# Layer 0: scores in four banks, two transpose banks and two rotating banks, with a new order of the row on every engine

## The chip, the cores and the metric

The kernel runs on one core of one Trainium2 chip. The metric is the time of one execution in microseconds of that core. The core has five engines with instruction queues of their own: TensorE (PE in the profile; its weight loads are PEld), VectorE (DVE), ScalarE (ACT), GpSimd (POOL) and SyncE (SP), which issues all DMA here. Each works through its queue in order; they meet only at semaphores. Matmuls write to PSUM, which has eight banks of 128 partitions by 512 float32; VectorE and ScalarE read them, GpSimd can't.

## What is computed

An image x of 128 channels by 256 by 256 goes through two residual layers, each behind a group normalisation. The change touches layer 0 alone: attention along each of the 256 rows of the image, with 4 heads of 64 channels, a bias per head, a gate and an output projection.

```python
x = (pair_rep - mu) * jax.lax.rsqrt(var + EPS) * ln_w + ln_b
q = proj(wq); k = proj(wk); v = proj(wv)          # (heads, 64, rows, 256)
g = jax.nn.sigmoid(proj(wg_w) + wg_b)
bias = jnp.einsum('hc,bcij->bhij', wb, x)
scores = jnp.einsum('bhcij,bhcik->bhijk', q, k) * scale + bias[:, :, None, :, :]
a = jax.nn.softmax(scores, axis=-1)
o = g * jnp.einsum('bhijk,bhcik->bhcij', a, v)
return jnp.einsum('oc,bcij->boij', wrep_w, o) + wrep_b
```

## The kernel before

The program has a first pass over the image (statistics and the bias parts, to about 426 us), layer 0, a short end of statistics, and layer 1. Layer 0 walks over the 256 image rows, W = 256 positions each, eight rows to an iteration of the loop (`UNROLL`). Every number of the products that feed scores is held as a high and a low part (float32r), and a product of two such numbers is three matmuls (`matmul_split`: high by high, low by high, high by low). One image row is:

- GpSimd: `normalise` parts 0 to 5, which subtract the mean, scale, weight, shift, and split into xn high and low; `divide`, which multiplies each head's exponents by the inverse of their sum. SyncE loads x, ln_w and ln_b in tiles of two rows into four buffers; a buffer is loaded again when its rows' y is done, since the residual reads x from it.
- TensorE: `queries`, `keys`, `values`, `gates` (6 matmuls of 128x256 each); `scores` per pair of heads (12 matmuls on half the array's height, two side by side); `transposes` per head (4 of 128x128); `attend` (8 matmuls in the program, 16 in the records, on half the array's width); `project_out` (6).
- ScalarE copies the high part of q and k (`queries_high`, `keys_high`), v (`values_out`), the tanh of the gates (`gates_out`), the high part of o, two heads' transposes, and the exponents with their sums.
- VectorE adds the bias to the scores and takes the maximum (`biased`), inverts the sums, subtracts for the low parts of q, k and o, copies two heads' transposes, multiplies by the gate (`gated`), adds the residual (`residual`, y) and measures y for the next statistics (`measure`). In the eight rows after iterations 7, 14, 21 and 28 it also joins the statistics of seven iterations (`join`).

The order on each engine is written by hand in its function `row(t, k, has)`: `scores(t, k + 2, 0)` in it means that in step k of the engine's walk the scores are those of image row k + 2. So each kind of work runs a fixed number of rows ahead, and the steps before row 0 and behind row 255 leave out what doesn't exist. The exponents lie in one buffer per head (`probs`), q, k, v, the gate and the transposed exponents in two each. The banks before: one for queries and values, one for keys and gates, two for scores (so the second pair of heads waits until the first pair has been read), two for transposes, one for attend, one for the output projection. A block's wait names who must have read its bank:

```python
for h in range(2):
    if pair:
        pe.wait_ge(s_ready[h], r + 1)
    else:
        wait(pe, s_ready[2 + h], r)
```

## Time and profile before

| | us |
|---|---|
| median of 3 runs (4820.17 to 4829.05) | 4822.93 |
| the profiled execution | 4825.53 |
| its span, first to last instruction | 4823.7 |
| TensorE busy, matmuls | 4606.1 (95%) |
| TensorE busy, weight loads | 3896.8 (81%) |
| VectorE busy | 3924.8 (81%) |
| ScalarE busy | 3768.1 (78%) |
| GpSimd busy | 3626.7 (75%) |
| TensorE's granted clock, mean | 0.975 of full speed |

The span is the profiled execution from its first instruction to its last; the execution's own time is 1.8 us longer. Busy shares are means over four stages with different limits, so what the change is worth has to be read inside layer 0, from about 440 to 2842 us. A granted clock of 1.00 is 2.4 GHz, 0.50 is 1.2 GHz. Idle time of an engine is printed behind an instruction in brackets with what ended it. A matmul's start is recorded and its end is modelled.

### The profile page before, as it was taken

What the parts mean: (1) busy time and instruction counts of PE and PEld (TensorE: products, weight loads), DVE (VectorE), ACT (ScalarE), POOL (GpSimd) and SP (SyncE); (2) the same over time, 40 slices, a digit from 0 to 9 for tenths busy, and PEclk for the clock granted to TensorE, in tenths of its full rate; (3) what the DMA queues carried; (4) which work ended last, traced back from release to release, by engine and by line L of the source; (5) the groups of instructions that cost most, each with busy time, mean ns of one, the idle gap of its engine ahead of it and who ended that gap; (6) DMA issues with size and microseconds to landing.
All of it is one profiled execution on the core that took longest, in us unless ns stands there. A gap on an engine that the chain in (4) does not pass through costs nothing. (4 is left out here: it accounts for less than half of the span.)

```text
span 4823.7 us, 153371 instructions
## 1 busy us (share of the span) xinstructions
PE 4606.1 (95%) x46135; PEld 3896.8 (81%) x46135; DVE 3924.8 (81%) x12976; ACT 3768.1 (78%) x11664; POOL 3626.7 (75%) x6054
## 2 busy tenths in 40 slices
PE   5667999999999999999999989999999999999998
PEld 1225888888888888888888868888888888888887
DVE  4444888889888988898888968888888888888887
ACT  2336888888888888888888868888888888888886
POOL 3443888888888888888888847777777777777776
PEclk8678999999999999999999989999999999999999
DMA  9996111111111111111111111111111111111111
GB/s 355 351 346 198 58 53 61 52 61 52 61 52 61 53 57 56 53 60 52 61 52 61 53 45 48 52 52 52 52 52 52 52 52 52 52 52 52 52 52 34
DMA packets 237387, 383.12 MB, mean 79 GB/s; under 512 B 18756, under 2 KB 156616, under 8 KB 224968
## 3 DMA queue, kind: packets, MB, share of 16 engines
q1 hardware_dynamic: 237256, 381.63, 23.3%
q8 instruction: 51, 0.84, 0.1%
q14 instruction: 80, 0.66, 0.0%
HBM read 309.21 MB, written 72.35 MB: 79 GB/s over the span
## 5 line engine op out<-in xcount | busy, mean ns | idle before, releaser
L1507 POOL TENSOR_SCALAR l_probs<-l_probs,l_inv 128x256 f32<-128x256 f32 x2048 | 941.5, 479 | 377.5 <-DVE l_inv L1404 377.5
L663 POOL TENSOR_SCALAR l_probs<-l_probs,l_inv 128x256 f32<-128x256 f32 x2048 | 947.8, 477 | 268.5 <-DVE l_inv L914 268.5
L832 ACT ACTIVATE l_probs<-l_probs,l_neg_max 128x256 f32<-128x256 f32 x2048 | 1021.0, 518 | 0.8 <-DVE l_neg_max L906 0.6
L1305 ACT ACTIVATE l_probs<-bank,l_neg_max 128x256 f32<-128x256 f32 x2048 | 942.5, 476 | 46.4 <-DVE l_neg_max L1398 39.4
L906 DVE CUSTOM_DVE_ANT_0 l_probs<-bank,bias 128x256 f32<-128x256 f32 x2048 | 779.9, 418 | 201.1 <-PE bank L773 197.1
L1411 DVE TENSOR_TENSOR l_probs_t<-bank,bias 128x512 f32<-128x512 f32 x1024 | 669.7, 685 | 131.0 <-PE bank L1217 116.0
L1398 DVE TENSOR_REDUCE l_neg_max<-bank 128x2 f32<-128x512 f32 x1024 | 675.0, 682 | 43.1 <-PE bank L1205 33.9
L773 PE MATMUL bank<-ident,l_probs 128*128 128x128 f32 x4096 | 629.5, 276 | 1.1 <-POOL l_probs L663 0.7
L1217 PE MATMUL bank<-ident,l_probs 128*128 128x128 f32 x4096 | 560.0, 274 | 5.3 <-POOL l_probs L1507 3.9
L786 PE MATMUL bank<-l_probs_t,l_v 128*64 128x256 f32 x4096 | 498.5, 385 | 0.2 <-issue 0.2
L773 PEld LDWEIGHTS bank<-ident,l_probs 128*128 128x128 f32 x4096 | 463.9, 141 | 36.8 <-POOL l_probs L663 1.7
L1217 PEld LDWEIGHTS bank<-ident,l_probs 128*128 128x128 f32 x4096 | 458.7, 141 | 25.1 <-POOL l_probs L1507 5.9
L872 ACT ACTIVATE l_probs_t<-bank 128x512 f32<-128x512 f32 x512 | 308.4, 602 | 212.7 <-PE bank L773 212.7
L832 ACT ACTIVATION_READ_ACCUMULATOR l_probs<-l_probs,l_neg_max 128x1 f32 x2048 | 428.9, 209 | 0.0
L1305 ACT ACTIVATION_READ_ACCUMULATOR l_probs<-bank,l_neg_max 128x1 f32 x2048 | 424.6, 207 | 0.0
L928 DVE COPY l_probs_t<-bank 128x512 f32<-128x512 f32 x512 | 350.1, 684 | 50.7 <-PE bank L773 50.5
L786 PEld LDWEIGHTS bank<-l_probs_t,l_v 128*64 128x64 f32 x4096 | 271.5, 136 | 143.4 <-issue 0.4
L675 POOL TENSOR_TENSOR l_xf<-l_x,mean 128x256 f32<-128x256 f32 x256 | 302.1, 1180 | 70.4 <-DMA l_ln_b<-in_L_conv_ln_b_dram 70.4
L97 PE MATMUL bank<-l_xn_high,wqk_high 128*128 128x256 f32 x1024 | 331.2, 323 | 14.4 <-POOL l_xn_low L690 14.1
L760 PE MATMUL bank<-l_k_high,l_q_high 64*128 64x256 f32 x2048 | 342.2, 331 | 1.5 <-DVE l_k_low L922 1.5
L531 POOL TENSOR_TENSOR fp_ln_w<-fp_x,fp_ln_w 128x2048 f32<-128x2048 f32 x32 | 144.3, 4509 | 219.1 <-PE bank L415 219.1
L760 PEld LDWEIGHTS bank<-l_k_high,l_q_high 64*128 64x128 f32 x2048 | 191.5, 184 | 142.4 <-issue 142.1
(205 smaller groups left out, 14710.2 us busy)
## 6 DMA issues: line engine op xcount, KB each, us to landing
fp_x<-in_x_dram SPq DMA_DIRECT2D x32, 1024.0 KB, 6.4
fp_ln_w<-in_L_conv_ln_w_dram SPq DMA_DIRECT2D x32, 1024.0 KB, 8.5
fp_ln_b<-in_L_conv_ln_b_dram SPq DMA_DIRECT2D x32, 1024.0 KB, 11.1
fp_pair<-in_L_conv_pair_repr_dram SPq DMA_DIRECT2D x32, 1024.0 KB, 10.6
l_x<-in_x_dram SPq DMA_DIRECT2D x128, 256.0 KB, 2.9
l_ln_w<-in_L_conv_ln_w_dram SPq DMA_DIRECT2D x128, 256.0 KB, 3.3
l_ln_b<-in_L_conv_ln_b_dram SPq DMA_DIRECT2D x128, 256.0 KB, 3.5
x<-l_y SPq DMA_DIRECT2D x128, 256.0 KB, 2.0
```

Source lines behind the costliest of these rows:

```text
L663: last = nc.gpsimd.tensor_scalar(probs[:, h, c], probs[:, h, c], inv[:, h, c:c + 1], 1.0, ALU.mult, ALU.mult)
L760: last = nc.tensor.matmul(b_s[j][:, c * W:(c + 1) * W], q[a][channels, k % 2, pair, c * P:(c + 1) * P], kk_[b][channels, k % 2, pair], sta ...
L773: last = nc.tensor.transpose(b_t[h % 2][:, kc * W + qc * P:kc * W + (qc + 1) * P], probs[:, h, qc, kc * P:(kc + 1) * P], m.ident[:])
L786: last = nc.tensor.matmul(b_av[D0 * j:D0 * (j + 1), pair * W:(pair + 1) * W], v[:, k % 2, kc, h * D0:(h + 1) * D0], probs_t[:, k % 2, h, k ...
L832: last = nc.scalar.activation(probs[:, h, c], probs[:, h, c], ACT.Exp, bias=neg_max[:, h, c:c + 1], scale=-1.0, accum_out=total[:, h, c:c ...
L906: last = nc.vector.tensor_tensor_reduce(out=probs[:, h, c], in0=b_s[h % 2][:, c * W:(c + 1) * W], in1=m.bias0[:, c, h], scale=-1.0, scalar ...
L928: nc.vector.tensor_copy(probs_t[:, k % 2, h], b_t[h % 2][:].rearrange("p (a c) -> p a c", a=KC)).then_inc(t_ready[h], 1)
L1217: last = nc.tensor.transpose(b_t[h % 2][:, kc * W + qc * P:kc * W + (qc + 1) * P], probs[:, h, qc, kc * P:(kc + 1) * P], m.ident[:])
L1305: last = nc.scalar.activation(probs[:, h, c], b_s[h % 4][:, c * W:(c + 1) * W], ACT.Exp, bias=neg_max[:, h, c:c + 1], accum_out=total[:, h ...
L1398: nc.vector.tensor_reduce(neg_max[:, h], b_s[h % 4][:].rearrange("p (a c) -> p a c", a=KC), AX.X, ALU.max, negate=True).then_inc(max_ready, 1)
L1411: nc.vector.tensor_tensor(probs_t[:, k % 2, h], b_t[h % 2][:].rearrange("p (a c) -> p a c", a=KC), m.bias1[:, :, h], ALU.add).then_inc(t_r ...
L1507: last = nc.gpsimd.tensor_scalar(probs[:, h, c], probs[:, h, c], inv[:, h, c:c + 1], 1.0, ALU.mult, ALU.mult)
```

## The change

Banks: four for scores, two for transposes, and two that rotate: queries, keys and the output projection share b_r[0]; values, gates and attend share b_r[1]. TensorE scores all four heads of a row in one stretch. Attend no longer stands behind the values but by itself between keys and transposes. Queries run four rows ahead of the output projection and keys five (both three before), GpSimd's first part seven rows (five before). Every engine has a new order. The numbers and shapes of the instructions stay the same. The lines of the kernel after are up to 33 lines further down than those of the same work before (L760 becomes L788, L773 L799, L786 L817).

The core of the diff (the other blocks' waits are changed in the same way; VectorE's and GpSimd's orders are new as a whole):

```diff
-    AHEAD = 5
+    AHEAD = 7
+    TURN_BANK = (0, 1, 0, 1)
+    TURNED_AHEAD = ((2, 1), (3, 1), (0, 0), (1, 0))
...
-        b_qv, b_kg = m.psum[0], m.psum[1]
-        b_s, b_t, b_av, b_out = m.psum[2:4], m.psum[4:6], m.psum[6], m.psum[7]
+        b_r, b_s, b_t = m.psum[0:2], m.psum[2:6], m.psum[6:8]
...
             def gates(t, k):
                 r = UNROLL * t + k
-                pe.wait_ge(k_ready, r + 1)
+                pe.wait_ge(xn_ready, r + 1)
+                if exists(r):
+                    pe.wait_ge(v_ready, r + 1)
...
             def scores(t, k, pair):
...
-                for h in range(2):
-                    if pair:
-                        pe.wait_ge(s_ready[h], r + 1)
-                    else:
-                        wait(pe, s_ready[2 + h], r)
+                for h in range(2 * pair, 2 * pair + 2):
+                    wait(pe, s_ready[h], r)
...
             def transposes(t, k, h):
...
-                if h >= 2:
-                    pe.wait_ge(t_ready[h - 2], r + 1)
-                else:
-                    wait(pe, t_ready[h + 2], r)
+                ahead, rows_back = TURNED_AHEAD[h]
+                wait(pe, t_ready[ahead], r + 1 - rows_back)
...
             def attend(t, k):
...
-                wait(pe, o_ready, r)
+                if exists(r + 1):
+                    pe.wait_ge(g_ready, r + 2)
...
             def project_out(t, k):
                 r = UNROLL * t + k
                 pe.wait_ge(o_split, r + 1)
-                wait(pe, y_ready, r)
+                if exists(r + 4):
+                    pe.wait_ge(q_ready, r + 5)
...
             def row(t, k, has):
-                if has(2):
-                    scores(t, k + 2, 0)
...
+                if has(4):
+                    queries(t, k + 4)
+                if has(2):
+                    values(t, k + 2)
                 if has(3):
-                    queries(t, k + 3)
...
+                    scores(t, k + 3, 0)
+                    scores(t, k + 3, 1)
                 if has(0):
                     project_out(t, k)
-                if has(3):
-                    values(t, k + 3)
+                if has(2):
+                    gates(t, k + 2)
+                    transposes(t, k + 2, 3)
+                    transposes(t, k + 2, 0)
+                if has(5):
+                    keys(t, k + 5)
                 if has(1):
                     attend(t, k + 1)
+                if has(3):
+                    transposes(t, k + 3, 1)
+                if has(2):
+                    transposes(t, k + 2, 2)
             rows(pe, row)
```

TensorE in the middle of an iteration before, from head 2's transposes (bank 4) over the keys to the scores; the brackets name the semaphores that an instruction waits for:

```order
L773 MATMUL bank4<-ident,l0_probs 128x128 [waits l0_t_ready0,l0_p_ready2]
L773 MATMUL bank4<-ident,l0_probs 128x128 x3
L97 MATMUL bank1<-l0_xn_high,wqk_high 128x256 [waits l0_g_ready,l0_xn_ready]
L98 MATMUL bank1<-l0_xn_low,wqk_high 128x256
L99 MATMUL bank1<-l0_xn_high,wqk_low 128x256
L97 MATMUL bank1<-l0_xn_high,wqk_high 128x256
L98 MATMUL bank1<-l0_xn_low,wqk_high 128x256
L99 MATMUL bank1<-l0_xn_high,wqk_low 128x256
L773 MATMUL bank5<-ident,l0_probs 128x128 [waits l0_t_ready1,l0_p_ready3]
L773 MATMUL bank5<-ident,l0_probs 128x128 x3
L760 MATMUL bank2<-l0_k_high,l0_q_high 128x256 [waits l0_s_ready0,l0_s_ready1,l0_k_ready,l0_q_ready]
```

And after, from the last matmul of the gates over the transposes of heads 3 and 0 and the keys to attend:

```order
L99 MATMUL bank1<-l0_xn_high,wg_t_low 128x256
L799 MATMUL bank7<-ident,l0_probs 128x128 [waits l0_t_ready1,l0_p_ready3]
L799 MATMUL bank7<-ident,l0_probs 128x128 x3
L799 MATMUL bank6<-ident,l0_probs 128x128 [waits l0_t_ready2,l0_p_ready0]
L799 MATMUL bank6<-ident,l0_probs 128x128 x3
L97 MATMUL bank0<-l0_xn_high,wqk_high 128x256 [waits l0_y_ready,l0_xn_ready]
L98 MATMUL bank0<-l0_xn_low,wqk_high 128x256
L99 MATMUL bank0<-l0_xn_high,wqk_low 128x256
L97 MATMUL bank0<-l0_xn_high,wqk_high 128x256
L98 MATMUL bank0<-l0_xn_low,wqk_high 128x256
L99 MATMUL bank0<-l0_xn_high,wqk_low 128x256
L817 MATMUL bank1<-l0_probs_t,l0_v 64x256 [waits l0_t_ready3,l0_v_ready,l0_t_ready2,l0_g_ready,l0_t_ready1,l0_t_ready0]
```

The transposes that stood apart stand in one stretch, and behind the keys comes attend, which waits for all four transposes, v, and the gates of the next row.

TensorE around the scores before, from the last matmuls of pair 0 on:

```order
L760 MATMUL bank3<-l0_k_low,l0_q_high 128x256
L760 MATMUL bank2<-l0_k_high,l0_q_low 128x256
L760 MATMUL bank3<-l0_k_high,l0_q_low 128x256
L773 MATMUL bank4<-ident,l0_probs 128x128 [waits l0_t_ready2,l0_p_ready0]
L773 MATMUL bank4<-ident,l0_probs 128x128 x3
L97 MATMUL bank1<-l0_xn_high,wg_t_high 128x256 [waits l0_k_ready]
```

And after, where pair 0 (banks 2 and 3) meets pair 1 (banks 4 and 5):

```order
L788 MATMUL bank3<-l0_k_low,l0_q_high 128x256
L788 MATMUL bank2<-l0_k_high,l0_q_low 128x256
L788 MATMUL bank3<-l0_k_high,l0_q_low 128x256
L788 MATMUL bank4<-l0_k_high,l0_q_high 128x256 [waits l0_s_ready2,l0_s_ready3,l0_k_ready,l0_q_ready]
L788 MATMUL bank5<-l0_k_high,l0_q_high 128x256
L788 MATMUL bank4<-l0_k_low,l0_q_high 128x256
```

Between the pairs stood transposes, gates, queries and keys; now pair 1 follows at once, in banks of its own.

ScalarE over most of a row before, from the value copy (L858) to head 1's exponents (L832):

```order
L858 ACTIVATE l_v<-bank 128x512 [waits l0_av_mm,l0_v_mm]
L872 ACTIVATE l_probs_t<-bank 128x512 [waits l0_av_mm,l0_t_mm0]
L865 ACTIVATE l_gate<-bank,wg_b_half 128x256 [waits l0_o_ready,l0_g_mm]
L865 ACTIVATE l_gate<-bank,wg_b_half 128x256
L852 ACTIVATE l_o_high<-l_o 128x512 [waits l0_out_mm,l0_o_ready]
L840 ACTIVATE l_q_high<-bank 128x512 [waits l0_s_mm1,l0_q_mm]
L872 ACTIVATE l_probs_t<-bank 128x512 [waits l0_av_mm,l0_t_mm2]
L832 ACTIVATE l_probs,l_total<-l_probs,l_neg_max 128x256 [waits l0_s_ready0]
L832 ACTIVATE l_probs,l_total<-l_probs,l_neg_max 128x256
L846 ACTIVATE l_k_high<-bank 128x512 [waits l0_s_mm1,l0_k_mm]
L832 ACTIVATE l_probs,l_total<-l_probs,l_neg_max 128x256 [waits l0_s_ready1]
```

And after, from the high part of o (L885) to the copy of a transpose (L905); L865 are now the exponents, L898 the gates:

```order
L885 ACTIVATE l_o_high<-l_o 128x512 [waits l0_o_ready]
L873 ACTIVATE l_q_high<-bank 128x512 [waits l0_s_mm1,l0_q_mm]
L865 ACTIVATE l_probs,l_total<-l_probs,l_neg_max 128x256 [waits l0_s_ready2]
L865 ACTIVATE l_probs,l_total<-l_probs,l_neg_max 128x256
L891 ACTIVATE l_v<-bank 128x512 [waits l0_av_mm,l0_v_mm]
L905 ACTIVATE l_probs_t<-bank 128x512 [waits l0_t_mm2]
L865 ACTIVATE l_probs,l_total<-l_probs,l_neg_max 128x256 [waits l0_s_ready1]
L865 ACTIVATE l_probs,l_total<-l_probs,l_neg_max 128x256
L898 ACTIVATE l_gate<-bank,wg_b_half 128x256 [waits l0_o_ready,l0_g_mm]
L898 ACTIVATE l_gate<-bank,wg_b_half 128x256
L905 ACTIVATE l_probs_t<-bank 128x512 [waits l0_av_mm,l0_t_mm0]
```

The gates' tanh stood right behind the first copy of a transpose; now it is the last of its step, behind head 1's exponents.

## Rows read from the trace of the kernel before

**Rows 1.** Stretches: busy us (instructions) of each engine; granted clock, DMA share, GB/s.

```profile
1000.00:2000.00 1000.00, 1000.00 (x9209) 851.97 (x9208) 884.75 (x3384) 848.16 (x2571) 861.36 (x1500) 1.00 0.17 57
1069.00:1144.00 75.00, 75.00 (x698) 63.95 (x694) 71.22 (x282) 63.75 (x193) 64.63 (x113) 1.00 0.17 56
```

**Rows 2.** TensorE's timeline over one row of layer 0: start, us, what.

```profile
1003.17 0.39 PE L760 MATMUL bank<-l_k_high,l_q_high 64*128 64x256 f32 x2
...
1003.40 0.28 PE L760 MATMUL bank<-l_k_low,l_q_high 64*128 64x256 f32 x2
...
1003.87 0.28 PE L760 MATMUL bank<-l_k_high,l_q_low 64*128 64x256 f32 x2
...
1004.08 0.66 PE L773 MATMUL bank<-ident,l_probs 128*128 128x128 f32 x4
...
1004.49 0.37 PE L97 MATMUL bank<-l_xn_high,wg_t_high 128*128 128x256 f32 x1
...
1005.29 0.60 PE L773 MATMUL bank<-ident,l_probs 128*128 128x128 f32 x4
...
1007.60 0.60 PE L773 MATMUL bank<-ident,l_probs 128*128 128x128 f32 x4
...
1008.13 0.39 PE L760 MATMUL bank<-l_k_high,l_q_high 64*128 64x256 f32 x2
...
1009.03 0.39 PE L97 MATMUL bank<-l_o_high,wrep_t_high 128*128 128x256 f32 x1
...
1009.85 0.29 PE L97 MATMUL bank<-wv_t_high,l_xn_high 128*128 128x256 f32 x1
...
1010.64 1.95 PE L786 MATMUL bank<-l_probs_t,l_v 128*64 128x256 f32 x16
...
1012.51 0.39 PE L760 MATMUL bank<-l_k_high,l_q_high 64*128 64x256 f32 x2
```

**Rows 3.** TensorE's timeline at the end of layer 0.

```profile
2826.63 1.04 PE L773 MATMUL bank<-ident,l_probs 128*128 128x128 f32 x8
...
2830.59 1.95 PE L786 MATMUL bank<-l_probs_t,l_v 128*64 128x256 f32 x16
...
2832.47 1.09 PE L773 MATMUL bank<-ident,l_probs 128*128 128x128 f32 x8
...
2840.55 0.38 PE L97 MATMUL bank<-l_o_high,wrep_t_high 128*128 128x256 f32 x1 [2.17 <-DVE l_o_low L941]
```

**Rows 4.** TensorE's timeline at the start of layer 0.

```profile
440.48 0.58 PE L97 MATMUL bank<-l_xn_high,wqk_high 128*128 128x256 f32 x1 [14.11 <-POOL l_xn_low L690]
...
448.53 0.36 PE L97 MATMUL bank<-l_xn_high,wqk_high 128*128 128x256 f32 x1 [0.32 <-ACT l_gate L865]
...
449.41 0.38 PE L760 MATMUL bank<-l_k_high,l_q_high 64*128 64x256 f32 x2
```

**Rows 5.** Groups by line, 1000 to 2600 us: busy us, mean ns | idle before.

```profile
L906 DVE CUSTOM_DVE_ANT_0 l_probs<-bank,bias 128x256 f32<-128x256 f32 x1372 | 522.4, 418 | 129.8 <-PE bank L773 129.5
...
L941 DVE TENSOR_TENSOR l_o_low<-l_o,l_o_high 128x512 fp32r<-128x512 f32 x171 | 149.4, 873 | 0.0
...
L865 ACT ACTIVATE l_gate<-bank,wg_b_half 128x256 f32<-128x256 f32 x342 | 143.5, 471 | 21.1 <-DVE l_o L936 1.0
...
L918 DVE TENSOR_TENSOR l_q_low<-bank,l_q_high 128x512 fp32r<-128x512 f32 x171 | 116.1, 679 | 0.0
...
L840 ACT ACTIVATE l_q_high<-bank 128x512 fp32r<-128x512 f32 x171 | 102.3, 598 | 0.0
```

**Rows 6.** ScalarE's timeline: the first exponent of two successive heads.

```profile
1504.17 0.53 ACT L832 ACTIVATE l_probs<-l_probs,l_neg_max 128x256 f32<-128x256 f32 x1
...
1505.15 0.51 ACT L832 ACTIVATE l_probs<-l_probs,l_neg_max 128x256 f32<-128x256 f32 x1
```

**Rows 7.** Line L628, the loads of ln_b: issue to landing.

```profile
DMA to landing us min/median/max: 3.3/3.5/6.5
```

**Rows 8.** Line L675, GpSimd's first subtraction: ns min/median/max, first and last start.

```profile
L675 POOL TENSOR_TENSOR l_xf<-l_x,mean x256: 722/1190/1197, 435.3 to 2800.8; 128x256 f32<-128x256 f32 x128
```

More of the change, by code:

```diff
@@ L980, in row @@
             def row(t, k, has):
+                if has(2):
+                    inverse(t, k + 2, 1)
+                    biased(t, k + 2, 3)
+                if has(1):
+                    transposed_out(t, k + 1, 3)
+                if has(2):
+                    biased(t, k + 2, 0)
+                if has(4):
+                    keys_low(t, k + 4)
                 if has(0):
```

186 lines of the change are left out of this document (100 added, 86 removed).

## The prediction

> **What bounds the kernel now.** I read first the busy times by stretch [rows 1]. In the middle of layer 0 TensorE (PE) is busy all of 1000 us at a granted clock of 1.00 (its upper level, 2.4 GHz), while VectorE has 885, ScalarE 848 and GpSimd 861. So TensorE sets the pace, and the reader should ask not who is waited for but what TensorE's own row is made of. A busy TensorE can still lose time between two kinds of matmul, because the ends of matmuls are modelled; only their starts can be trusted. Therefore I read next TensorE's timeline over one row of the image and took differences of starts [rows 2]. One row takes 1012.51 - 1003.17 = 9.34 us. Its twelve blocks, from one block's first matmul to the next block's:
>
> scores pair 0 0.91; transposes 0.41; gates 0.80; transposes, queries, transposes and keys together 2.31 (twice 1.16: with 0.80 for the projection, as for the gates, 0.36 for four transposes); transposes 0.53; scores pair 1 0.90; output projection 0.82; values 0.79; attend 1.87. They add up to 9.34.
>
> None of these rows has an idle time with a releaser behind it, so no semaphore holds TensorE here. But equal work costs unequal time. Four transposes take 0.36 when a projection follows, and 0.53 when scores follow. A score block has 6 slots (a slot is a pair of matmuls that run side by side); from the second to the sixth slot the starts are (1003.87 - 1003.40)/4 = 0.12 apart, so six slots are 0.71 us, yet the block takes 0.91: its first slot takes 0.23, and its last 0.21. What TensorE loses is at the borders between full-height matmuls (projections, transposes), half-height ones (scores, 64*128) and half-width ones (attend, 128*64). A border between projection and transposes costs nothing: the 1.16 are 6 slots of 0.12 and 4 transposes of 0.11 (eight were busy 1.04 where four would be 0.60 [rows 2, 3]).
>
> **The change, part by part.** The matmuls are the same in number and shape; only their order and their banks differ. So the sum is the sum of the borders. The new row on TensorE is Q V S0 S1 P G T3 T0 K A T1 T2 (letters as above; K keys, A attend). Priced from rows:
>
> - Q after transposes, before a projection: 0.80, as the gates [rows 2].
> - V followed by scores. Values followed by attend took 0.79 [rows 2]; a projection followed by scores took 449.41 - 448.53 = 0.88 with the first slot's shift of 0.09 that a block behind transposes has in the record [rows 4]. The two agree: 0.79.
> - S0 and S1 in one stretch: 0.91 + 6 slots of 0.12 = 1.61. No stretch of twelve slots of this shape is in the trace. Bounds: nothing saved, 1.81; all saved, 1.61. I take 1.61, since slots inside a block are already at 0.12.
> - P after scores 0.82 [rows 2]; G straight after P, six slots 0.71.
> - T3 and T0 in one stretch: four more are 1.04 - 0.60 = 0.44, so 0.36 + 0.44 = 0.80.
> - K after transposes and before attend: 0.80 + 0.09 for the border = 0.89 (as projection to scores, above).
> - A followed by transposes: 2832.47 - 2830.59 = 1.88 [rows 3].
> - T1 and T2 behind A, before Q: 0.41 + 0.44 = 0.85.
>
> Sum 0.80 + 0.79 + 1.61 + 0.82 + 0.71 + 0.80 + 0.89 + 1.88 + 0.85 = 9.15, and 9.12 if each block is taken a hundredth smaller, where the records are rounded; I take 9.13. That is 0.21 us less per row, **54 us over 256 rows**. Bounds of this term: if a long score stretch saves nothing 0.01 x 256, about 3 us; if every price is 0.01 high, 62 us.
>
> The Trainium skill ("TensorEngine Tiling (Array Packing)", section Key Properties) says that changing the tiling mode, not merely the tile, drains TensorE. By that rule one counts borders: A to S, S to T, T to S, S to P and V to A before (5); V to S, S to P, K to A and A to T afterwards (4). The row's loss is 9.34 less 8.4 of plain slots (42 of 0.12, 16 transposes of 0.11, attend's 1.87 without its 0.2 border). A fifth of that, 0.19 us per row, would be 49 us; the rows, priced one by one, give 54, and I go by the rows.
>
> **What must stay hidden.** A saved border is only a gain if no semaphore takes its place. Four banks go to scores, so queries, keys and the output projection share one bank, and values, gates and attend another; each block now waits until its predecessor's result has been read out. I laid the new row out from the prices above, with Q starting at 0: V 0.80, S0 1.59, P 3.20, G 4.02, T3 4.73, K 5.52, A 6.41, T1 8.28, next Q 9.13. A matmul is in the bank 0.28 us after its start [rows 2].
>
> - Q to P: Q is complete at 0.96, ScalarE copies 0.60 and VectorE subtracts 0.68 [rows 5], done at about 2.3 to 2.5; P starts at 3.20. In between VectorE has only the output subtraction to finish first (0.87). Slack about 0.7.
> - P to K: P complete at 4.2, VectorE's residual is shorter than that subtraction, 0.5; K at 5.52. Slack 0.8.
> - V to G: V complete at 1.67. ScalarE has the query copy, then one head's exponents (1505.15 - 1504.17 = 0.98 [rows 6]), then the value copy: 1.0 + 0.5 + 1.0 + 0.6 = 3.1; G at 4.02. Slack 0.9.
> - G to A: G complete at 4.89; the gates' tanh takes two activations of 0.47, overlapped, 0.85: 5.75 against 6.41. **This is the tightest, 0.6 us**, and on ScalarE's queue the tanh now stands behind the exponents of head 1 of the row after next. Those wait for VectorE's biased scores of head 1 (two of 0.42), which wait for S0, complete at 2.56: 2.56 + 0.84 + 0.98 = 4.4 with latencies near 4.6, before 4.89.
> - A to V and K to Q: one VectorE operation of 0.68, and a copy and a subtraction, against 1.6 and 2.7 us; slack 0.8 and 1.1.
>
> The other engines' floor: per 9.34 us row VectorE is busy 8.27, ScalarE 7.92, GpSimd 8.05 (each sum of [rows 1] over the 107 rows in 1000 us). All lie under 9.13. In the eight rows after a joining point VectorE is busy 71.22 of 75 us, 8.87 per row, still under 9.13. So TensorE remains the bound.
>
> **Seven rows of lead** costs at the ends. Before, TensorE's first matmul of the layer is at 440.48 and its last block starts at 2840.55 [rows 3, 4]: 2401 us with the last block, against 256 x 9.34 = 2391. Fill and drain cost 10 us for a lead of three rows from the first projection to the output projection; now it is five (keys run five rows ahead). Bounds: nothing, if the early keys fit into gaps, and two whole rows, 18 us. The first transposes now follow the first scores inside one iteration, so a whole chain of biased scores, exponents, inverse and division (near 3 us) lies bare at least twice: I take 10. The loads: a buffer is free when its rows' residuals are done, and its next first use is now two rows earlier. Landing takes 3.5 us in the median and 6.5 at most [rows 7], behind about 1.6 of issues on SP's queue; by my layout the first subtraction comes about 6 us after the residual. Tight, but GpSimd can be an operation late without TensorE noticing. I price it at nothing; if the cover is gone, every second row would cost up to 1 us.
>
> **Sum.** 54 less, 10 more: 44 us off. The profiled execution took 4825.5 us with a span of 4823.7; the median of the runs shown is 4822.9, half a part in a thousand away. From the median I get **4779 us**. Its own range is 4768 to 4796.
>
> **Rivals.**
>
> 1. *A new wait eats part of the gain* (0.13). The margins of 0.6 to 0.9 us were computed with engines free when needed. VectorE runs at 8.27/9.13 = 91% and ScalarE at 87%; against it speaks that all four rings have slack. With a wait of 0.05 to 0.13 us per row the time would be 4792 to 4812.
> 2. *GpSimd and VectorE get into each other's way.* The row of GpSimd's first subtraction shows it: 0.72 us at best, 1.19 in the median [rows 8], because it overlaps VectorE's output subtraction (L941, 0.87 against L918's 0.68, which reads a bank). In the new order that subtraction meets other GpSimd operations, perhaps two of them. Twice 0.47 us more puts GpSimd at 9.0 per row, still under 9.13: no change in time up to there; at three times, 9.5, the row would be GpSimd's and the kernel 40 us slower than before, near 4865 (0.03). The Trainium skill ("SBUF — State Buffer", section "SBUF: two separate sides") calls the shared port pair an exclusive lock that a VectorE operation with two SBUF inputs takes against a GpSimd one; the trace's 1.19 against 0.72 agrees.
> 3. *The gates' eviction comes late, and it is slower* (0.07). Place: attend waits for the tanh, which stands behind head 1's exponents, behind the biased scores, behind S0 of the same iteration. That is a loop through TensorE; each us by which it passes A's start at 6.41 is a us of row. With 0.6 of slack, it decides when the chain is 0.6 + 0.21 = 0.8 us longer than I worked out. At 1.1 us longer the row is 9.63, and the kernel 4823 + 0.29 x 256 + 10 = 4907.
> 4. *No change* (0.05): the long score stretch saves its border, but the waits put the same 0.2 back; 4814 to 4832.
>
> **How the numbers follow.** My forecast holds 0.72, rival 1 0.13, the two slower cases together 0.10, no change 0.05. This kernel cannot be told from itself within 0.2%, 10 us. Faster by more than that: 0.72 and most of rival 1, 0.83; same 0.06; slower 0.11. The range takes my own and most of rival 1: 4766 to 4808.
>
> **What would show it.** TensorE's starts in the row: 9.13 us from Q to Q; scores as twelve slots, 1.61; 0.44 more for paired transposes; no idle time with a releaser in front of P, G, K or A. Wrong would be: a row of "PE waits for the gate's activation" or "for y" of tens of us; GpSimd's subtraction (L675's successor) much over 1.19; waits for the loads of ln_b; more than 20 us between layer 0's length and 256 rows. Layer 1 and the first pass must stay within a microsecond or two.

## The result: 36.8 us off, and the profile after

| | before | after |
|---|---|---|
| median of 4 runs, us | 4823.89 (4820.17 to 4829.05) | 4787.05 (4786.48 to 4792.58) |
| ratio, 95% interval | | 0.9925 (0.9911 to 0.9938) |
| span of the profiled execution | 4823.7 | 4784.8 |
| TensorE's granted clock, mean | 0.975 | 0.976 |
| layer 0, first matmul to last output projection | 440.48 to 2840.55: 2400.1 | 437.77 to 2801.36: 2363.6 |
| from there to the end of the span | 1983.2 | 1983.4 |

The 36.5 us that layer 0 is shorter are the whole difference of the medians, 36.8. The two profiled spans differ by 38.9, because layer 0 also began 2.7 us earlier in the second of them. I forecast 44 off (4779, range 4766 to 4808).

TensorE's timeline of the kernel after, over one row, in order Q V S0+S1 P G T K A T:

```profile
1000.67 0.36 PE L97 MATMUL bank<-l_xn_high,wqk_high 128*128 128x256 f32 x1
...
1001.46 0.28 PE L97 MATMUL bank<-wv_t_high,l_xn_high 128*128 128x256 f32 x1
...
1002.25 0.38 PE L788 MATMUL bank<-l_k_high,l_q_high 64*128 64x256 f32 x2
...
1003.87 0.39 PE L97 MATMUL bank<-l_o_high,wrep_t_high 128*128 128x256 f32 x1
...
1004.68 0.28 PE L97 MATMUL bank<-l_xn_high,wg_t_high 128*128 128x256 f32 x1
...
1005.39 1.04 PE L799 MATMUL bank<-ident,l_probs 128*128 128x128 f32 x8
1006.18 0.36 PE L97 MATMUL bank<-l_xn_high,wqk_high 128*128 128x256 f32 x1
...
1007.07 1.95 PE L817 MATMUL bank<-l_probs_t,l_v 128*64 128x256 f32 x16
1008.95 1.09 PE L799 MATMUL bank<-ident,l_probs 128*128 128x128 f32 x8
1009.80 0.36 PE L97 MATMUL bank<-l_xn_high,wqk_high 128*128 128x256 f32 x1
```

Differences of starts: Q 0.79, V 0.79, scores 1.62, P 0.81, G 0.71, T3 T0 0.79, K 0.89, A 1.88, T1 T2 0.85. That is 9.13 where it was 9.34 [rows 2]. From one row's output projection to the next one's, over some 50 rows without a wait, it is 9.127 us against 9.340 before, so 0.213 less per row and 54.4 us over the 255 rows between the first output projection and the last. The two transpose blocks and the two score blocks no longer have a border between them, and no start here has a releaser behind it.

Layer 0 should then have become 54.4 us shorter, and was 36.5. The 17.9 us between are in two places. The first is in the waits of 460 to 2760 us (engine, line, releaser: us in all, times, longest); TensorE had none of over 0.1 us there before:

```profile
POOL l_probs L664 <- DVE l_inv L947: 267.5, 303, 2.0
...
PE bank L799 <- DVE l_probs_t L961: 7.4, 4, 2.0
POOL l_xf L676 <- DMA l_ln_b<-in_L_conv_ln_b_dram: 1.8, 2, 1.3
```

One line of them is TensorE's: four waits in front of head 3's transposes, at 1062.30, 1575.61, 2088.73 and 2601.88 us, 7.4 us in all. The first of them in TensorE's timeline:

```profile
1060.03 0.28 PE L99 MATMUL bank<-l_xn_high,wg_t_low 128*128 128x256 f32 x1
1062.30 1.06 PE L799 MATMUL bank<-ident,l_probs 128*128 128x128 f32 x8 [1.99 <-DVE l_probs_t L961]
```

The row is longer by more than this idle time, which is counted from a modelled end. Its output projection and the next one's start at

```profile
1058.63 0.39 PE L97 MATMUL bank<-l_o_high,wrep_t_high 128*128 128x256 f32 x1
...
1070.02 0.39 PE L97 MATMUL bank<-l_o_high,wrep_t_high 128*128 128x256 f32 x1
```

which is 11.39 us instead of 9.13. The other three such rows take 11.35, 11.17 and 11.18, and the four together cost 8.6 us, not 7.4.

TensorE waits for a bank that VectorE empties (L961). VectorE's timeline at the same place:

```profile
1058.16 0.43 DVE L939 CUSTOM_DVE_ANT_0 l_probs<-bank,bias 128x256 f32<-128x256 f32 x1
1058.51 0.08 DVE L939 DVE_READ_ACCUMULATOR2_ANT l_neg_max<- 128x1 f32 x1
1061.11 0.42 DVE L939 CUSTOM_DVE_ANT_0 l_probs<-bank,bias 128x256 f32<-128x256 f32 x1 [2.51 <-issue]
1061.46 0.08 DVE L939 DVE_READ_ACCUMULATOR2_ANT l_neg_max<- 128x1 f32 x1
1061.46 0.69 DVE L961 COPY l_probs_t<-bank 128x512 f32<-128x512 f32 x1
```

VectorE stands still for 2.51 us between the two halves of head 1's biased scores. The last matmul of those scores started at 1057.70, so they were complete when the gap began at 1058.60, and "issue" says that nothing shown held VectorE. All four gaps (2.51, 2.48, 2.28, 2.29) come 7 us after VectorE leaves its loop for one of the four iterations that are written out because they join statistics (the first exit is at 1051.61). Before, VectorE had such gaps too, and they hit nobody:

```profile
1067.94 0.48 DVE L965 BATCH_NORM_STATS2 chunk_stats<-l_y 128x6 f32<-128x64 f32 x3
1069.36 0.23 DVE L965 BATCH_NORM_STATS2 chunk_stats<-l_y 128x6 f32<-128x64 f32 x1 [0.94 <-issue]
```

The second place is the ends. The first output projection comes 36.75 us after the first matmul (474.52 - 437.77); before, 26.84. That is 9.9 more for the fill, and by the balance (17.9 - 8.6 - 9.9) 0.6 less for the drain. The stretches of the fill, of the kernel after and then of the kernel before (columns as in [rows 1]):

```profile
440.00:450.00 10.00, 6.07 (x30) 5.34 (x32) 2.62 (x4) 2.41 (x5) 6.37 (x11) 0.50 0.50 160
450.00:460.00 10.00, 8.09 (x77) 7.11 (x76) 6.54 (x30) 8.14 (x26) 7.11 (x14) 0.95 0.01 2
```

```profile
440.00:450.00 10.00, 9.07 (x58) 8.11 (x60) 3.54 (x11) 5.52 (x12) 8.29 (x13) 0.69 0.70 234
450.00:460.00 10.00, 8.46 (x82) 7.50 (x80) 6.92 (x30) 9.02 (x29) 7.65 (x15) 1.00 0.01 2
```

TensorE is busy 6.07 of 10 us where it was 9.07 (5.49 and 9.55 in the first ten us from each one's first matmul), and its granted clock is at the lower level (1.2 GHz) for all of that stretch. From the first matmul on, the lower level lasts 13 us in the kernel after and 6 in the kernel before. TensorE's waits in the fill, 438 to 470 us:

```profile
PE bank L97 <- DVE l_k_low L955: 3.4, 3, 1.5
...
PE bank L799 <- POOL l_probs L664: 2.1, 2, 1.5
PE bank L97 <- DVE l_q_low L951: 1.5, 1, 1.5
```

The first and the third are projections that wait for the low part of k or q: queries, keys and output projection share one bank, and at the start there is no other work to put between them. The second are transposes that wait for the divided exponents, the chain that lies bare. At the drain the last output projections wait for the low part of o, at 2789.23, 2796.33 and 2801.36 us (0.85, 1.58, 2.18), where before only the last one did [rows 3]. By the balance the drain is no longer than before all the same. The whole balance: -54.4 + 8.6 + 9.9 - 0.6 = -36.5.

### The profile page after: what moved, and what is told of

It reads as the page before. It is cut to its first block and busy times, and to the rows that moved or that the text cites. A ratio compares the mean times of both kernels' runs of the same rounds, so it can differ in the third digit from the quotient of the medians.

```text
span 4784.8 us, 154166 instructions
## 1 busy us (share of the span) xinstructions
PE 4548.7 (95%) x46135; PEld 3884.5 (81%) x46135; DVE 3951.4 (83%) x12976; ACT 3860.5 (81%) x11664; POOL 3617.1 (76%) x6054
## 5 line engine op out<-in xcount | busy, mean ns | idle before, releaser
L865 ACT ACTIVATE l_probs<-l_probs,l_neg_max 128x256 f32<-128x256 f32 x2048 | 1016.0, 499 | 20.8 <-DVE l_neg_max L939 13.8
L1249 PE MATMUL bank<-ident,l_probs 128*128 128x128 f32 x4096 | 559.8, 274 | 5.3 <-POOL l_probs L1539 3.9
L799 PE MATMUL bank<-ident,l_probs 128*128 128x128 f32 x4096 | 546.1, 276 | 9.7 <-DVE l_probs_t L961 7.4
L799 PEld LDWEIGHTS bank<-ident,l_probs 128*128 128x128 f32 x4096 | 450.2, 141 | 109.2 <-issue 106.8
L817 PE MATMUL bank<-l_probs_t,l_v 128*64 128x256 f32 x4096 | 498.5, 385 | 0.4
L1249 PEld LDWEIGHTS bank<-ident,l_probs 128*128 128x128 f32 x4096 | 458.6, 141 | 25.1 <-POOL l_probs L1539 5.9
L817 PEld LDWEIGHTS bank<-l_probs_t,l_v 128*64 128x64 f32 x4096 | 271.9, 136 | 145.7 <-issue 1.1
L865 ACT ACTIVATION_READ_ACCUMULATOR l_probs<-l_probs,l_neg_max 128x1 f32 x2048 | 388.5, 190 | 0.0
L961 DVE COPY l_probs_t<-bank 128x512 f32<-128x512 f32 x512 | 351.6, 687 | 0.3 <-PE bank L799 0.3
L676 POOL TENSOR_TENSOR l_xf<-l_x,mean 128x256 f32<-128x256 f32 x256 | 273.0, 1066 | 71.7 <-DMA l_ln_b<-in_L_conv_ln_b_dram 71.7
L788 PE MATMUL bank<-l_k_high,l_q_high 64*128 64x256 f32 x2048 | 316.3, 306 | 0.0
L905 ACT ACTIVATE l_probs_t<-bank 128x512 f32<-128x512 f32 x512 | 304.4, 594 | 10.5
L97 PE MATMUL bank<-l_xn_high,w_qk_high 128*128 128x256 f32 x1024 | 301.0, 294 | 2.4 <-ACT l_xf L1372 1.9
```

Of the source, the lines that this page charges most:

```text
L97: nc.tensor.matmul(out, lh, rh, start=start, stop=False)
L799: last = nc.tensor.transpose(b_t[TURN_BANK[h]][:, kc * W + qc * P:kc * W + (qc + 1) * P], probs[:, h, qc, kc * P:(kc + 1) * P], m.ident[:])
L817: last = nc.tensor.matmul(b_r[1][D0 * j:D0 * (j + 1), pair * W:(pair + 1) * W], v[:, k % 2, kc, h * D0:(h + 1) * D0], probs_t[:, k % 2, h, ...
L865: last = nc.scalar.activation(probs[:, h, c], probs[:, h, c], ACT.Exp, bias=neg_max[:, h, c:c + 1], scale=-1.0, accum_out=total[:, h, c:c ...
L961: nc.vector.tensor_copy(probs_t[:, k % 2, h], b_t[TURN_BANK[h]][:].rearrange("p (a c) -> p a c", a=KC)).then_inc(t_ready[h], 1)
L1249: last = nc.tensor.transpose(b_t[h % 2][:, kc * W + qc * P:kc * W + (qc + 1) * P], probs[:, h, qc, kc * P:(kc + 1) * P], m.ident[:])
```

## The experiments

Unless said otherwise, all change the kernel after. "Length" is layer 0 from its first matmul to the start of the last output projection, 2363.6 us in the kernel after; "first projection" is the time from the first matmul to the first output projection, 36.75 us there. What a gap "costs" is by how much the rows around it are longer than 9.127 us, from start to start. "Ratio" is to the kernel before, run beside it.

**a0_after: the same kernel again.**

> The changed kernel once more, beside the kernel before on the same chip. Theory (borders between tiling shapes on TensorE): 9.125 us from queries to queries, 4787 us within 5, ratio 0.991 to 0.994. Four TensorE waits of about 1.9 us in front of the transposes of head 3, each behind a VectorE gap of 2.3 to 2.5 us eight or nine us after VectorE has left its loop.

4793.49 us (4789.06 to 4794.57), ratio 0.9933 (0.9917 to 0.995). The time is 1.5 us above the expected range, the ratio inside it. The same four waits, 7.4 us in all, which cost 8.6; length 2365.0. Layer 0 began at 441.03 instead of 437.77, since the first pass took longer. That start lies between 435.8 and 443.0 in the runs of this study, so a time here can move by 7 us with nothing changed in layer 0, and lengths of layer 0 are the finer measure.

They have a noise of their own, in the fill. TensorE's clock reaches its upper level 13 us after the first matmul in both runs, but here it falls again 3 us later. The stretch from 16 to 20 us after the first matmul, here and in the kernel after:

```profile
457.03:461.03 4.00, 3.62 (x18) 3.19 (x18) 2.50 (x10) 3.02 (x12) 3.92 (x8) 0.61 0.01 4
```

```profile
453.77:457.77 4.00, 3.62 (x38) 3.29 (x40) 2.75 (x11) 3.69 (x14) 3.92 (x8) 1.00 0.02 4
```

The first projection comes at 38.18 instead of 36.75, and that is the whole 1.4 us by which the length differs. The clock fell this second time in a0, e2, e4, e5 and e8 (first projection 37.8 to 38.3), and not in the kernel after, e3 and e6 (36.8). What decides it no run shows. So a length is compared below with that of a run whose fill went the same way.

**e1_values_between: the values between the two pairs of scores.** Two borders come back, everything else stays.

```diff
                     queries(t, k + 4)
+                if has(3):
+                    scores(t, k + 3, 0)
                 if has(2):
                     values(t, k + 2)
                 if has(3):
-                    scores(t, k + 3, 0)
                     scores(t, k + 3, 1)
```

> Only TensorE's order differs from the changed kernel: values stand between the scores of heads 0 and 1 and those of heads 2 and 3, so the long score stretch is cut and TensorE passes two more borders per row. Banks, waits and every other engine's order stay. Theory A (the gain is borders saved): queries before scores 0.88 instead of 0.79, two score blocks of 0.91 instead of one of 1.62, values 0.90 instead of 0.78; the row 9.125 + 0.09 + 0.20 + 0.12 = 9.53 us, the kernel 4787 + 0.41 x 256 = 4891 us, slower than the kernel before by about 1.4%. Rival B (the gain comes from the four score banks, which take a wait away): the row stays near 9.13, the kernel within 10 us of 4787.

4882.24 us (4881.07 to 4883.59), ratio 1.012 (1.0103 to 1.0137); length 2457.3. TensorE's timeline over the part that changed:

```profile
1004.48 0.36 PE L97 MATMUL bank<-l_xn_high,wqk_high 128*128 128x256 f32 x1
...
1005.36 0.39 PE L788 MATMUL bank<-l_k_high,l_q_high 64*128 64x256 f32 x2
...
1006.27 0.39 PE L97 MATMUL bank<-wv_t_high,l_xn_high 128*128 128x256 f32 x1
...
1007.16 0.38 PE L788 MATMUL bank<-l_k_high,l_q_high 64*128 64x256 f32 x2
...
1008.07 0.39 PE L97 MATMUL bank<-l_o_high,wrep_t_high 128*128 128x256 f32 x1
```

Q 0.88, S0 0.91, V 0.89, S1 0.91: together 3.59, and 3.20 in the kernel after. The same 24 slots (6 + 6 + 12), without a wait, cost 0.39 us more, because four borders between full-height and half-height matmuls lie in them instead of two. A row takes 9.513 (9.53 expected). So it is the borders that the change saves; a score block of its own costs 0.387 us a row (9.513 - 9.127), 98.6 over 255 rows, of which 4.3 come back because VectorE's gaps cost 4.3 instead of 8.6; that leaves 94.3 against the 93.7 by which layer 0 is longer.

**e2_join_out: without the join, the iterations still written out.**

```diff
-                if isinstance(t, int) and t - 1 in JOINED:
+                if False:
```

> The changed kernel without the joining of statistics (the 128 aggregations that merge seven iterations' statistics are left out, so layer 1's mean and deviation are not the reference's), but VectorE still leaves its loop at the same four places. Theory C (the four waits on TensorE come from instruction fetch after VectorE leaves its loop): four VectorE gaps of 2.3 to 2.5 us and four TensorE waits of 1.8 to 2.0 us stay; layer 0 is as long as before within 1 us. Rival D (they come from the extra 0.8 us of VectorE work per row in the eight rows of a join): the waits vanish, layer 0 is 7 us shorter.

4789.98 us in one run; length 2366.4. The first gap is still there, in the same operation:

```profile
1062.73 0.42 DVE L939 CUSTOM_DVE_ANT_0 l_probs<-bank,bias 128x256 f32<-128x256 f32 x1 [2.58 <-issue]
```

TensorE waits 6.2 us in all. An iteration written out is 32 instructions shorter without the join, and the later gaps (1584.05, 2103.71, 2622.04) don't stay at the same place in the row, though that was expected. The four end 9.4, 15.8, 22.4 and 27.5 us behind their exits. Each falls 5 to 7 us later than the one before, and 32 instructions are about 6 us of VectorE's row (391 instructions to eight rows of 9.127 us). So the place goes by the count of instructions, and the joining work is not the cause.

**e3_no_exits: without the join, and VectorE never leaves its loop before the last iteration.** As e2, and:

```diff
-            rows(dve, row, hinted=nc, stops=[last + 1 for last in JOINED])
+            rows(dve, row, hinted=nc)
```

> As the run without the joining (that work is left out here too), but VectorE stays in one loop from iteration 1 to 30 and never leaves it in between. Theory C (instruction fetch after leaving the loop): no VectorE gap over 1 us in the middle of layer 0, no TensorE wait there, layer 0 shorter by 7.4 us, the kernel near 4779. Rival D (extra VectorE work): the same as the run before this one, which then has no waits either.

4783.17 us (4780.01 to 4785.16), ratio 0.9913 (0.9896 to 0.9929); length 2357.0, 6.6 less than that of the kernel after, whose fill went the same way (8.1 less than a0_after's). The stretch 1000 to 2000 us shows no TensorE idle time at all (996.07 busy in the kernel after):

```profile
1000.00:2000.00 1000.00, 1000.00 (x9428) 867.47 (x9429) 907.70 (x3395) 907.59 (x2632) 879.80 (x1534) 1.00 0.18 57
```

One gap is left, behind the one exit that is left; VectorE's timeline and TensorE's:

```profile
2740.24 0.42 DVE L939 CUSTOM_DVE_ANT_0 l_probs<-bank,bias 128x256 f32<-128x256 f32 x1 [2.30 <-issue]
```

```profile
2741.42 1.07 PE L799 MATMUL bank<-ident,l_probs 128*128 128x128 f32 x8 [1.76 <-DVE l_probs_t L961]
```

This one costs 2.0 us; the 6.6 are the rest of the 8.6. So leaving the loop makes the gap. What remained open was why it sits 31 instructions behind the exit here and 42 behind it before.

**e4_pad245: 245 empty instructions ahead of VectorE's loop.**

```diff
+            for _ in range(245):
+                dve.nop(nofuse=True)
             rows(dve, row, hinted=nc, stops=[last + 1 for last in JOINED])
```

> The changed kernel with 245 empty instructions on VectorE ahead of layer 0's first row, where VectorE has nothing to do for 30 us. In the program VectorE's code ahead of the loop is 412 instructions in the changed kernel and 401 in the kernel before, and each loop and exit together are 769, three blocks of 256 and one; so the gap of 2.5 us behind head 1's biased scores and the gap of 0.9 us in the measuring instructions, about 11 instructions later in the row, would be the same block border. 245 more are 11 fewer modulo 256. Theory C (a block border of VectorE's code after leaving the loop): the four gaps move about 11 instructions later, to the end of VectorE's row (residual or measure), and become about 1 us; TensorE waits at most 0.5 us at each; layer 0 is 5 to 7 us shorter than 2363.6. Rival (the gap belongs to the instruction or its wait): it stays in head 1's biased scores at 2.3 to 2.5 us.

4790.11 us (4786.31 to 4794.32), length 2364.8, TensorE waits of 7.1 us, and VectorE's gaps where they were. The built program doesn't contain the empty instructions: it has 412 instructions ahead of the loop, as without them. So it says nothing on its question, and is one more repetition of the kernel after.

**e5_slot0, e6_slot110, e8_slot79: where VectorE's loop stands in the code.** `head_slot` puts the loop's first instruction on the given slot of a block of 256 instructions. In the built programs layer 0 has 412 VectorE instructions ahead of the loop, and 401 before, since the longer fill writes out more rows. The loop's body has 391 instructions; if the gap is a block border, it sits 512 - 391 - slot instructions behind the exit: 121 for slot 0, 42 for 79, 31 for 90, 11 for 110. Slot 90 for the kernel after and slot 79 for the kernel before are worked out backwards, from gaps that stand 31 and 42 instructions behind the exit; the count confirms only that they are 11 apart. The three loops put on a given slot are the test.

```diff
-        with hinted.Fori(done, stop, engines=[engine.engine], hint_back_edge=True) as t:
+        with hinted.Fori(done, stop, engines=[engine.engine], hint_back_edge=True, head_slot={engine.engine: 79}) as t:
```

> The changed kernel with each VectorE loop of layer 0 placed at the first slot of a block of 256 instructions. A loop of 391 instructions then ends at slot 135, so the next border comes 121 instructions, 2.6 rows or about 23 us, after leaving the loop. Theory C: the gaps move to about 23 us after the exit, and if the fetch begins with the exit they are gone; layer 0 shorter by 5 to 7.4 us in that case, else the same. Entering the loop by a branch may cost a gap of its own at each of five loops, 1 to 2 us of VectorE, partly hidden. Rival (extra work of a join): no gap moves.

> As the run with slot 0, but each loop starts at slot 110 and ends at slot 245 of the next block: the border comes 11 instructions after the exit, in the first biased scores of the row. Theory C: the four gaps stand there, still over 2 us; TensorE has more slack behind that place (the scores of head 3 are needed 3.5 us before anything waits), so its waits are shorter than 1.9 us, 0.5 to 1.5. Rival: gaps stay in head 1's biased scores.

> The changed kernel with each VectorE loop of layer 0 placed at slot 79 of a block of 256 instructions. Counted in the program, the gaps so far stand at instruction 1810 + 391 + 42 = 2243 of VectorE's code in the kernel before and at 1821 + 391 + 31 = 2243 in the changed one: the same border, 42 instructions behind the exit before (in the measuring instructions, gap 0.9 us) and 31 now (2.3 to 2.5 us). Slot 79 puts it 42 instructions behind the exit again. Theory C1 (the size of the gap, too, comes from the place in the row): gaps of about 1 us in the measuring instructions, TensorE waits 0.3 us or less at each, layer 0 6 to 7.4 us shorter than 2363.6 to 2365. Theory C2 (only the place follows, the fetch takes its 2 us or more): gaps stay at 1.4 to 2.5 us, TensorE waits 0.8 to 1.8 us in front of queries or values, layer 0 shorter by 0 to 4 us.

VectorE's timelines show the first gap of slot 0, of slot 110, and of slot 79:

```profile
1082.29 0.69 DVE L951 TENSOR_TENSOR l_q_low<-bank,l_q_high 128x512 fp32r<-128x512 f32 x1 [1.59 <-issue]
```

```profile
1053.86 0.08 DVE L939 DVE_READ_ACCUMULATOR2_ANT l_neg_max<- 128x1 f32 x1 [2.13 <-issue]
```

```profile
1066.22 0.23 DVE L998 BATCH_NORM_STATS2 chunk_stats<-l_y 128x6 f32<-128x64 f32 x1 [0.78 <-issue]
```

| slot | end of the gap behind the exit | gaps in VectorE | they cost TensorE | length; first projection | time (ratio) |
|---|---|---|---|---|---|
| 0 | 25.5 us | 1.36 to 1.59 | 4.1, and 2.0 at the entry | 2362.4; 38.26 | 4787.51 (0.9922; 0.9906 to 0.9939) |
| 110 | 4.2 | 1.87 to 2.28 | 6.1 | 2361.1; 36.76 | 4783.27, one run |
| 79 | 9.8 | 0.73 to 1.03 | 3.1, and 1.9 at the entry | 2361.5; 38.15 | 4787.07 (0.992; 0.9904 to 0.9937) |
| 90 (after) | 9.5 | 2.28 to 2.51 | 8.6 | 2363.6; 36.75 | 4787.05 (0.9925) |

The gap went where the count puts it in all three. On slot 79 it is in the same instruction as in the kernel before (the last of `measure`'s four) and as short. The 6 to 7.4 us less that were expected of it did not come: the length is 2.1 less. In e5 and e8 a gap appears that the kernel after doesn't have, at the entry into the first loop (2.77 and 2.69 us), and in both the clock fell a second time in the fill. With these two counted the lengths follow: 4.1 + 2.0 + 1.5 (38.26 - 36.75) are 1.0 less than 8.6, and the length is 1.2 less; 3.1 + 1.9 + 1.4 are 2.2 less, and it is 2.1; 6.1 is 2.5 less, and it is 2.5. The times of the four can't be told apart.

**e7_spare_banks: the first two rows' keys in score banks that stand empty then.**

```diff
+        def keys_bank(t, k):
+            r = UNROLL * t + k
+            return b_s[2 + r] if isinstance(r, int) and r < 2 else b_r[0]
...
-                if exists(r):
+                if isinstance(r, int) and r < 2:
+                    wait(pe, q_ready, r)
+                elif exists(r):
                     pe.wait_ge(k_ready, r + 1)
...
+                if pair and isinstance(r, int) and r == 0:
+                    pe.wait_ge(k_ready, 2)
```

> The changed kernel, but keys of rows 0 and 1 go to two score banks that are still unused, so that the first queries and keys needn't take turns in one bank. Theory (a third of the 11.6 us that the ends cost more comes from this taking of turns, and from the low clock meanwhile): the first output projection comes 33 to 35 us after layer 0's first matmul instead of 36.7, layer 0 is 2 to 4 us shorter, the steady rows stay at 9.125. Rival (the chain of head 1's scores, exponents and division bounds the start): under 1 us.

4790.81 us in one run, with layer 0 starting late at 443.01; first projection 34.0, 2.8 less; length 2362.5, 1.1 less, where 2 to 4 were expected. The rest went back in one row: behind the 2.03 us wait at 1064.83, the clock fell.

```profile
1064.00:1066.00 2.00, 1.17 (x11) 1.21 (x12) 1.97 (x11) 1.81 (x6) 0.94 (x2) 1.00 0.01 4
1066.00:1068.00 2.00, 2.00 (x12) 1.31 (x12) 2.00 (x11) 1.65 (x5) 1.18 (x3) 0.54 0.00 0
1068.00:1070.00 2.00, 2.00 (x12) 0.95 (x8) 1.22 (x5) 1.62 (x7) 1.18 (x2) 0.60 0.00 0
```

For about 4 us the mean granted clock is 0.54 and 0.60, though TensorE is busy throughout, and the row takes 12.95 us. The next such wait of the same run, 2.06 us at 1579.77, is no shorter; behind it the clock stayed up, and the row takes 11.47:

```profile
1580.00:1582.00 2.00, 2.00 (x20) 1.72 (x20) 1.97 (x13) 1.81 (x6) 1.04 (x3) 1.00 0.00 0
```

So the fall cost 1.5 us. In e2 the same is seen behind its first wait, of 2.05 us:

```profile
1066.00:1068.00 2.00, 2.00 (x10) 1.16 (x12) 1.48 (x6) 1.91 (x7) 1.45 (x3) 0.50 0.00 0
```

The 2.8 us understate the bank. In this run's fill the clock reached the upper level after 9 us and fell again (mean 0.57 from 455 to 459 us), so that it is to be set beside the fills in which the clock fell as well, 38.2: 4.2 less. In e10, below, the clock stayed up, and the first projection comes 4.0 earlier than the 36.75 of the kernel after:

```profile
450.05:454.05 4.00, 3.62 (x38) 3.29 (x40) 2.75 (x11) 3.70 (x14) 3.92 (x8) 1.00 0.02 4
```

The shared bank accounts for about 4 of the fill's 9.9 us, the longer time at the lower clock included.

**e9_gate_twice: the gates' tanh computed twice,** the first time into a buffer that nobody reads: rival 3's chain made longer by two activations.

```diff
-                for c in range(HC):
-                    last = nc.scalar.activation(gate[:, k % 2, c], b_r[1][:, c * W:(c + 1) * W], ACT.Tanh, bias=m.wg_b_half[:, c:c + 1], scale=0.5)
+                for to in (spare, gate):
+                    for c in range(HC):
+                        last = nc.scalar.activation(to[:, k % 2, c], b_r[1][:, c * W:(c + 1) * W], ACT.Tanh, bias=m.wg_b_half[:, c:c + 1], scale=0.5)
```

> The changed kernel with the gates' tanh worked out twice, first into a spare buffer that nobody reads, then as before: 0.73 us more on ScalarE between the end of the gates' matmuls and attend. In the changed kernel's trace the tanh is done about 0.63 us before attend starts. Theory (each ring has the slack of its layout, and the gates' is 0.6): attend waits 0.10 to 0.20 us in every row for ScalarE, the row is 9.22 to 9.33 us, the kernel 4812 to 4840 us. Rival (the queues are so full that any added work shows at once): 0.73 us or more per row, 4970 us. Rival (slack far larger than worked out): no change, 4787.

4850.43 us (4845.55 to 4852.35), ratio 1.005 (1.0033 to 1.0067); length 2429.0. Its waits, 1000 to 2600 us:

```profile
PEld bank L818 <- issue: 59.1, 175, 0.4
...
PE bank L818 <- ACT l_gate L900: 28.2, 169, 0.2
```

Attend (L818) waits for the gate in every row, and its own first weight load is late as well. Keys to attend takes 1.120 us instead of 0.884, so 0.24 per row and 60 to 65 us in all, above the 0.10 to 0.20 and the 4812 to 4840 us expected. Added were 0.73 us of ScalarE, so the slack in the kernel after is about 0.49.

**e10_slot79_spare: slot 79 and the spare banks together.** The edits of e8 and e7.

> Both mends together: the VectorE loops at slot 79, and keys of rows 0 and 1 in unused score banks. With theory C1 layer 0 is 8 to 10 us shorter than 2363.6 to 2365 (6 to 7.4 from the exits, 2.8 from the start), with C2 3 to 7; the kernel 4777 to 4784 us.

4779.93 us (4779.11 to 4781.38), ratio 0.9908 (0.9891 to 0.9924). It is the fastest of the study, 7 us under the kernel after, and inside the expected range. Length 2355.8 (7.8 less), first projection 32.76 (4.0 less). Its stretch and one of its waits, 460 to 2760 us:

```profile
1000.00:2000.00 1000.00, 999.25 (x9418) 866.22 (x9417) 914.01 (x3456) 908.82 (x2627) 880.19 (x1533) 1.00 0.17 57
```

```profile
PE bank L806 <- DVE l_probs_t L968: 1.8, 3, 1.5
```

The line has only the idle times over 0.15 us in front of the transposes. By the rows' lengths, what is left of the gaps costs TensorE about 0.7 us at each of the four exits and 2.0 at the entry into the first loop.

## Why the prediction was right, and where it was not

**The borders: right, and to size.** "54 us over 256 rows" measured 54.4, and no block is more than 0.014 us from its price. The Trainium skill ("TensorEngine Tiling (Array Packing)", section Key Properties) says that a change of the tiling mode drains TensorE. Counting borders by that gave 49; but the row's plain slots (42 of 0.12, 16 of 0.11 and 1.67) add up to 8.47 and not 8.4, so that it gives 45, the sign and most of the size. Two side sums were off too: a hundredth off each of nine blocks is 9.06 and not 9.12, and prices 0.01 high would have been worth 77 us and not 62. The forecast uses neither. The long score stretch, whose bounds were 1.61 and 1.81, is 1.62. e1 is the test: two borders put back, and the row is 0.39 us longer, without a wait in it.

**The ends: right in size, and for the most part by another cause.** "I take 10", bounds 0 to 18; 9.3 measured, 9.9 more in the fill and 0.6 less in the drain. The reason given, a bare chain of biased scores, exponents, inverse and division, is one part (transposes wait 2.1 us for it in the fill). Another was not named: the rotating bank between queries and keys, about 4 us (e7, e10), and with it the lower clock, which lasted 13 us from the first matmul instead of 6. That the sum came to 10 is in part luck.

**The rings: right.** No P, G, K or A waits in the steady state. The gates' slack, "the tightest, 0.6 us", is 0.49 by e9; the other slacks were not tested. Rival 3 wanted a chain 0.8 us longer for the whole gain to go. By e9 it is 0.7 (0.49 and the 0.21 gained per row), and with 0.73 more on ScalarE the kernel was no longer faster than before (ratio 1.005).

**The step that failed: the iterations written out.** I wrote of the eight rows after a joining point that VectorE "is busy 71.22 of 75 us, 8.87 per row, still under 9.13. So TensorE remains the bound." The sum of busy time is right and e2 shows that the joining costs nothing. But I had counted work alone. VectorE's row in the trace of before also had the 0.94 us gap at 1069.36, behind its loop's exit. The change lengthens the code of VectorE's fill by 11 instructions, so that the gap falls into a block of head 1's biased scores, ahead of a copy that TensorE needs; it grows to 2.3 to 2.5 us there, and costs 8.6 in layer 0. The ends cost 0.7 less than the 10, and the borders gave 0.4 more than the 54, so the forecast missed layer 0 by 7.5 (44 against 36.5).

**Rival 1** (a new wait) came true in a form that it did not have: 8.6 us, which is 0.03 per row, but in four places of 2 us and none in the ring. **Rival 2** (GpSimd and VectorE in each other's way) did not come. GpSimd is busy 8.0 us per row, as before, and its first subtraction has a median of 1170 ns against 1190 [rows 8]. In the kernel after 195 of the 256 overlap VectorE's output subtraction and take 1.17 us, and the 61 that don't take 0.73; before, 251 overlapped it:

```profile
L676 POOL TENSOR_TENSOR l_xf<-l_x,mean x256: 722/1170/1173, 432.6 to 2753.9; 128x256 f32<-128x256 f32 x128
```

**The loads** at nothing: right; GpSimd waits for ln_b twice, 1.8 us in all, and nobody waits for GpSimd then. **Layer 1** did not move (1983.2 and 1983.4 us from layer 0's last output projection to the end). The first pass ended 2.7 us earlier, more than the "microsecond or two" allowed, but its end moves by 7 us between runs in which it is the same. "More than 20 us between layer 0's length and 256 rows" would have counted against me, and does: it is 2363.6 + 0.8 for the last block - 2336.4 = 28.0. The bound left no room, since it was the 10 of before and the 10 more of the forecast. What lies above it is the 8.6 of the gaps, less the 0.7 by which the ends stayed under 10.

**What stays open.** Why a gap is 0.9 us on slot 79 and 2.3 on slot 90. The transfers of instructions show the form of it. GB/s in 40 slices of 0.05 us, and the queue, of the kernel before from 1067 and of the kernel after from 1058 us:

```profile
GB/s 0 0 0 0 0 0 0 0 0 0 0 164 0 0 0 0 0 0 0 0 0 0 0 0 0 0 0 0 0 0 0 0 0 0 0 0 0 0 0 0
...
q14 instruction: 1, 0.01, 1.6%
```

```profile
GB/s 0 0 0 0 0 0 0 0 0 0 0 0 0 0 0 0 0 0 0 0 0 0 164 0 0 0 0 0 0 0 0 0 0 0 0 0 0 0 0 0
...
q14 instruction: 1, 0.01, 1.8%
```

The packet comes at 1067.57 before, 0.85 us ahead of the moment at which VectorE runs dry (1069.36 - 0.94), and at 1059.13 after, 0.5 us behind it. From the packet to VectorE's next instruction it is 1.79 us before, 1.98 after, and 1.72 to 1.94 at the exits of e5, e6 and e8. So what differs is when the packet comes, not how long it takes. That semaphore waits keep VectorE's sequencer from running ahead to the border in the one place and not in the other is my reading, and no run isolates it.

## What to carry to other kernels

Where TensorE is busy all the time and waits for nobody, take differences of starts and price the borders between tiling shapes; here that sum was good to 1 us in 54, and one ring's slack, worked out from operation times, was good to 0.1 us. When a loop is left for iterations that are written out, look in the trace for a gap of "issue" on that engine behind each exit, and see what will stand there afterwards: what is added to or taken from the code ahead of the loop moves it. Price a wait, too, from start to start: here four waits of 7.4 us in the brackets made their rows 8.6 us longer. Test a slack by adding work to its chain rather than by arguing that it is there, and compare lengths of the stage that was changed where another stage's length varies by as much as the effect. Look at the granted clock in both runs before you do.

## What the runs showed of the hardware

- **Leaving its loop cost VectorE 0.7 to 3.0 us, some way behind the exit**, once for each exit. In e5, e8 and e10 there was a gap at the entry into the first loop as well (2.7 to 2.8), directly behind the row ahead of it. The place behind the exit follows the count of instructions modulo 256 in four placements of the loop (4.2, 9.5, 9.8 and 25.5 us behind the exit) and in e2's shorter iterations, and a packet on the instruction queue stands at each. The Trainium skill ("Runtime: NRT & Kernel Launch", section "Instruction fetch mechanics") says that an engine fetches its code in blocks of 256 instructions, one block ahead, and that a taken branch out of this window breaks it. The block's size agrees; the stall of the exits comes at the first border behind the exit and not at the branch.
- **Two borders more cost 0.39 us** between full-height and half-height matmuls (e1). At each border 0.09 of it is at the end of the block before and 0.11 in the first slot behind.
- **Four times TensorE's clock fell after a wait in the middle of layer 0**: behind 2.03 us in e7, 2.05 in e2, and 2.12 and 2.03 in e9 the granted clock was 0.50 for two to three us, though TensorE had gone back to work; in e7 that cost 1.5 us. Behind waits as long, 2.06 us in e7 and 2.04 in a0, it stayed at 1.00, and so it did behind the four of 1.75 to 1.99 us in the kernel after. So the length of the wait alone doesn't decide it.
- **The same code can start at two speeds**: in five of the runs with the kernel after's fill the clock fell a second time 15 to 18 us after the first matmul, which cost 1.0 to 1.5 us; in three it did not.
